# The decay of a Mamba recurrence in a ring of three PSUM banks, with softplus summed by TensorE and three B products lent to GpSimd

## Chip, cores, metric

One Trainium2 chip, one core. The metric is the device time of the whole program in microseconds, the median of the runs; lower is better.

## What is computed

The program runs two layers over a batch of 4 images (128 channels, 64 x 64 = 4096 positions). Layer 0 sorts patches by a score, projects them, runs a selective state-space recurrence and sorts them back; layer 1 is attention over normalised queries and keys, and a mixture of experts. The change touches the recurrence alone and the projection ahead of it:

```python
dbc = xc @ x_proj_w.T                       # dt_low (8), B (16), C (16) for each position
dt = jax.nn.softplus(dt_low @ dt_proj_w.T + dt_proj_b)
dA = jnp.exp(dt[..., None] * A)             # 256 channels x 16 states
dBx = dt[..., None] * Bc[:, :, None, :] * xc[..., None]
h = dA_t * h + dBx_t                        # over 4096 positions
y_t = einsum('bds,bs->bd', h, C_t)
y = y + D * xc;  y = y * silu(z)
```

## The kernel before

A loop over the 4 images runs seven stages; each stage is a block in which every engine has its own instruction queue, tied to the others by counting semaphores. An engine works its queue strictly in order.

The recurrence (`scan`) holds the 256 channels as two halves of 128 partitions and the positions as 8 chunks of 512 columns. Per image it goes over the chunks, in each over the 16 states, and in each state over the two halves. One state takes:

- TensorE (L846, L850) spreads row B of this state over 128 partitions into a PSUM bank, and row C into another, from three bf16 pieces that add up to the fp32 value;
- ScalarE (L870) makes the decay exp(dt x A) of each half in PSUM: four banks, so that decay s, h may be written once the scan of two states before has read its bank; then it copies C to SBUF (L873);
- VectorE (L923, `inject`) multiplies u = dt x xc (SBUF) by B (PSUM) for both halves, 1024 columns, and runs the hardware scan of each half (L941). The queue's order is scan of half 0, injection of the next state, scan of half 1;
- GpSimd (L898) keeps the last column of h for the next chunk, and (L901) multiplies h by C into a separate buffer `g`;
- TensorE (`total`, L838) adds these products into the two Y banks by identity matmuls, four states late, and opens each chunk with two matmuls of D (L836). All of these are fp32, two passes each;
- VectorE's `finish` (L929) multiplies Y by silu(z), once a chunk, after state 2 of the next.

Beside this, the steps of the next chunk are made in between (`Steps`): the dt projection (L593), |v| and relu(v) (L600, L601), exp(-|v|) (L605), 1 + e (L610), a rounding rest on VectorE (L626), Ln (L614, with a table load before and another at the next decay), two GpSimd passes that make softplus (L646, L650), GpSimd's u (L653), and the bf16 pieces: ScalarE high (L617) and middle (L621), GpSimd remainder (L636) and low (L640). For chunk 0 the same steps are made inside the stage before, `project`, in which the input projections (L682, L685), a four-tap convolution on VectorE (L760, L763), Silu (L710, L716) and the x projection (L676) go over the chunks.

The functions that the diff touches:

Of the kernel before, what the change touches and what calls it, by code (L numbers as in the profile page):

```python
# [16 lines left out]
HD = DI // 128  # L17
# [542 lines left out]
class Steps:  # L560
# [4 lines left out]
    def __init__(self, k, dt_banks):  # L565
        self.k, self.dt_banks = k, dt_banks
        at = [STEPS_AT]

        def take(cols):
            at[0] += cols  # L570
            return k.at(at[0] - cols, cols)

        self.dt, self.u = [take(HD * CH) for _ in range(2)], [take(HD * CH) for _ in range(2)]
        self.ab, self.onep, self.rx = take(HD * CH), take(HD * CH), take(HD * CH)
        self.rest = self.onep[:, 0:CH]
# [4 lines left out]
        (self.dt_mm, self.ab_s, self.e_s, self.w_s, self.q_s, self.ln_s, self.rx_s, self.l1_s, self.dt_s, self.hi_s, self.mid_s,  # L580
         self.r_s, self.pc_s) = (k.sem(n) for n in (
             "dt_mm", "dt_abs", "dt_exp", "dt_onep", "dt_rest", "dt_ln", "dt_relu", "log1p", "dt_ready", "high_ready",
             "middle_ready", "remainder", "pieces_ready"))

    def credit_first(self, eng):

        for s, n in ((self.dt_mm, HD), (self.ab_s, 2), (self.e_s, 1), (self.w_s, 1), (self.q_s, 1), (self.ln_s, 1), (self.rx_s, 2),
                     (self.l1_s, 1), (self.dt_s, 2), (self.hi_s, 1), (self.mid_s, 1), (self.r_s, 1), (self.pc_s, 1)):
            eng.sem_inc(s, n)

    def tensor_dt(self, pe, c, h):
        k = self.k
        pe.matmul(k.bank(self.dt_banks[h]), k.dtw[:, h * 128:(h + 1) * 128], self.dbc[:, cols_of(c)], start=True, stop=True)\  # L593
            .then_inc(self.dt_mm, 1)

# [11 lines left out]
    def scalar_one_plus(self, act, c):  # L607
        act.wait_ge(self.e_s, c + 1)
        act.wait_ge(self.pc_s, c + 1)
        act.activation(self.onep, self.ab, ACT.Identity, bias=self.k.cols[:, C_ONE:C_ONE + 1]).then_inc(self.w_s, 1)  # L610

    def scalar_log(self, act, c):
        act.wait_ge(self.q_s, c + 1)
        act.activation(self.onep, self.onep, ACT.Ln).then_inc(self.ln_s, 1)  # L614

# [6 lines left out]

    def vector_rounding(self, dve, c):

        dve.wait_ge(self.w_s, c + 1)
        dve.scalar_tensor_tensor(self.ab, self.onep, 1.0, self.ab, ALU.subtract, ALU.subtract).then_inc(self.q_s, 1)  # L626
# [15 lines left out]
    def pool_softplus(self, pool, c, q, part):  # L642

        if part == 0:
            self.pool_wait(pool, self.ln_s, c + 1)
            pool.tensor_tensor(self.onep, self.onep, self.ab, ALU.subtract).then_inc(self.l1_s, 1)  # L646
        if part == 1:
            self.pool_wait(pool, self.l1_s, c + 1)
            self.pool_wait(pool, self.rx_s, c * 2 + 2)
            pool.tensor_tensor(self.dt[q], self.onep, self.rx, ALU.add).then_inc(self.dt_s, 1)  # L650
        if part == 2:
            self.pool_wait(pool, self.dt_s, c * 2 + 1)
            pool.tensor_tensor(halves(self.u[q]), halves(self.dt[q]), self.xc[:, :, cols_of(c)], ALU.mult).then_inc(self.dt_s, 1)  # L653


def project(k):
# [12 lines left out]
    with nc.Block() as block:  # L669
        @block.tensor  # L670
        def _(pe):
# [16 lines left out]
            for c in range(1, 4):  # L688
# [6 lines left out]
            with pe.Fori(4, NCH) as c:  # L695
                inproj(c)
                xproj(c - 1)
# [3 lines left out]
        def _(act):  # L701
# [40 lines left out]
            steps.scalar_one_plus(act, 0)  # L742
            k.ready_table(act, ACT.Silu, 2)
            with act.Fori(4, NCH - 2) as c:
                body(c)
            steps.scalar_log(act, 0)
            body(NCH - 2)
            body(NCH - 1)
# [4 lines left out]
        def _(dve):  # L753
# [13 lines left out]
            with dve.Fori(0, 5) as c:  # L767
                convolve(c)
            steps.vector_rounding(dve, 0)
            with dve.Fori(5, NCH) as c:  # L770
                convolve(c)

        @block.gpsimd
        def _(pool):
# [4 lines left out]
            for part in range(3):  # L779
                if part == 2:  # L780
                    steps.pool_wait(pool, xc_s, HD)
                steps.pool_softplus(pool, 0, 0, part)
# [8 lines left out]
def scan(k):  # L791
# [5 lines left out]
    B_BANK, C_BANK, DA_BANK, Y_BANK = 0, 1, 2, 6  # L797
    steps = Steps(k, (C_BANK, C_BANK))
# [3 lines left out]
    dbx, hb, g = low[0:2], low[2:6], low[6:10]  # L802
    cs = [low[10 + i // 2][:, (i % 2) * CH:(i % 2 + 1) * CH] for i in range(4)]
    assert steps.end <= ARENA
    dt, u, pieces, dt_s, rx_s, pc_s = steps.dt, steps.u, steps.pieces, steps.dt_s, steps.rx_s, steps.pc_s

    b_mm, c_mm, y_mm, da_s, dbx_s, sc_s, hl_s, hc_s, cs_s, fin_s = (k.sem(n) for n in (
        "b_mm", "c_mm", "y_mm", "da_ready", "dbx_ready", "scan_done", "hlast_saved", "hc_ready", "c_copied", "chunk_done"))

    def da(s, h):  # L810

        return k.bank(DA_BANK + HD * (s % 2) + h)
# [15 lines left out]
    with nc.Block() as block:  # L828
        @block.tensor
        def _(pe):  # L830
            def total(c, s):
                pe.wait_ge(hc_s, c * DS + (s + 5))
# [4 lines left out]
                for h in range(HD):  # L837
                    last = pe.matmul(k.bank(Y_BANK + h), k.ident[:, :], halves(g[s % 4])[:, h, :], start=False, stop=s == DS - 1)  # L838
                last.then_inc(y_mm, 1)

            def body(c, q, more):
                pe.wait_ge(pc_s, c + 1)
                for s in range(DS):
                    n = c * DS + s
                    pe.wait_ge(dbx_s, n + 1)
                    pe.matmul(k.bank(B_BANK), k.sel[:, s, :], pieces[q], start=True, stop=True).then_inc(b_mm, 1)  # L846
                    pe.wait_ge(cs_s, n + 1)
                    if more and 1 <= s <= HD:
                        pe.wait_ge(rx_s, c * HD + (s + HD))
                    pe.matmul(k.bank(C_BANK), k.sel[:, DS + s, :], pieces[q], start=True, stop=True).then_inc(c_mm, 1)  # L850
                    if s >= 4:
                        total(c, s - 4)
                    elif not first(c):
                        total(c - 1, s - 4 + DS)
                    if more and s < HD:
                        pe.wait_ge(cs_s, n + 2)
                        steps.tensor_dt(pe, c + 1, s)
            chunks(body, pe)
            for s in range(DS - 4, DS):
# [3 lines left out]
        def _(act):  # L863
            def body(c, q, more):
                act.wait_ge(dt_s, c * 2 + 1)
                for s in range(DS):
                    n = c * DS + s
                    for h in range(HD):
                        act.wait_ge(sc_s, c * (2 * DS) + (2 * s + h + 5))
                        act.activation(da(s, h), halves(dt[q])[:, h, :], ACT.Exp, scale=k.amat[:, h, s:s + 1]).then_inc(da_s, 1)  # L870
                    act.wait_ge(c_mm, n + 1)
                    act.wait_ge(hc_s, n + 1)
                    act.activation(cs[s % 4], k.bank(C_BANK), ACT.Copy).then_inc(cs_s, 1)  # L873


                    if more and s == 0:
                        steps.scalar_high(act, c + 1, 1 - q)
                    if more and s < HD:
                        steps.scalar_abs(act, c + 1, s)
                    if more and s == 2:  # L880
                        steps.scalar_exp(act, c + 1)
                    if more and s == 3:
                        steps.scalar_middle(act, c + 1, 1 - q)
                    if more and s == 7:
                        steps.scalar_one_plus(act, c + 1)
                    if more and s == 10:
                        steps.scalar_log(act, c + 1)
            chunks(body, act)

        @block.gpsimd  # L890
        def _(pool):
# [3 lines left out]
            def body(c, q, more):  # L895
                for s in range(DS):
                    wait(sc_s, c * (2 * DS) + (2 * s + 2 + 8))
                    pool.tensor_copy(k.hlast[:, s, :, :], halves(hb[s % 4])[:, :, CH - 1:CH]).then_inc(hl_s, 1)  # L898
                    wait(cs_s, c * DS + (s + 2))
                    wait(y_mm, c * DS + (s + 1))  # L900
                    pool.tensor_tensor(halves(g[s % 4]), halves(hb[s % 4]), cs[s % 4].unsqueeze(1).broadcast_to([128, HD, CH]),  # L901
                                       ALU.mult).then_inc(hc_s, 1)
                    if more and s == 0:
                        steps.pool_remainder(pool, c + 1, 1 - q)
                    if more and s == 5:
                        steps.pool_low(pool, c + 1, 1 - q)
                    if more and s in (10, 11, 12):
                        steps.pool_softplus(pool, c + 1, 1 - q, (10, 11, 12).index(s))

            pool.memset(k.hlast[:, :, :, :], 0.0).then_inc(k.sem("h_zero"), 1)  # L910
            pool.wait_ge(k.sem("h_zero"), 1)
            pool.sem_inc(hl_s, DS)
            pool.sem_inc(hc_s, 4)
# [3 lines left out]
        def _(dve):  # L917
            def inject(c, q, s):
                if s == 0:
                    dve.wait_ge(dt_s, c * 2 + 2)  # L920
                dve.wait_ge(b_mm, c * DS + (s + 1))
                dve.wait_ge(sc_s, c * (2 * DS) + (2 * s + 6))
                dve.tensor_tensor(halves(dbx[s % 2]), halves(u[q]), k.bank(B_BANK).unsqueeze(1).broadcast_to([128, HD, CH]),  # L923
                                  ALU.mult).then_inc(dbx_s, 1)

            def finish(c):

                dve.wait_ge(y_mm, c * DS + (DS + 4))
# [3 lines left out]
            def body(c, q, more):  # L932
                inject(c, q, 0)
                for s in range(DS):
                    n = c * DS + s
                    dve.wait_ge(hl_s, n + (DS - 3))
                    dve.wait_ge(hc_s, n + 1)
                    dve.wait_ge(dbx_s, n + 2)
                    for h in range(HD):
                        dve.wait_ge(da_s, c * (2 * DS) + (2 * s + h + 1))  # L940
                        dve.tensor_tensor_scan(halves(hb[s % 4])[:, h, :], da(s, h), halves(dbx[s % 2])[:, h, :],  # L941
                                               k.hlast[:, s, h, :], ALU.mult, ALU.add).then_inc(sc_s, 1)
                        if h == 0 and s < DS - 1:
                            inject(c, q, s + 1)
                    if more and s == 8:
                        steps.vector_rounding(dve, c + 1)
                    if s == 2 and not first(c):
# [4 lines left out]
            dve.sem_inc(cs_s, 1)  # L952
            dve.sem_inc(sc_s, 8)
            dve.sem_inc(fin_s, 1)
            dve.sem_inc(y_mm, 4)
# [771 lines left out]
```

## Time and profile before

| | us |
|---|---|
| median of 3 runs (range) | 5882.98 (5876.63 to 5884.37) |
| the profiled execution, its time | 5884.61 |
| its span | 5882.9 |
| VectorE busy | 5070.9 (86%) |
| TensorE busy | 4708.2 (80%) |
| ScalarE busy | 3751.1 (64%) |
| GpSimd busy | 1666.3 (28%) |
| mean granted TensorE clock | 0.940 of full |

Times are microseconds from the span's start. PE is TensorE, DVE VectorE, ACT ScalarE, POOL GpSimd. Busy shares are over the whole program; the recurrence is four stretches of some 475 us, one for each image. The first runs from about 222 to 698.

### The profile page before, as it was taken

What the parts mean: (1) busy time and instruction counts of PE and PEld (TensorE: products, weight loads), DVE (VectorE), ACT (ScalarE), POOL (GpSimd) and SP (SyncE); (2) the same over time, 40 slices, a digit from 0 to 9 for tenths busy, and PEclk for the clock granted to TensorE, in tenths of its full rate; (3) what the DMA queues carried; (4) which work ended last, traced back from release to release, by engine and by line L of the source; (5) the groups of instructions that cost most, each with busy time, mean ns of one, the idle gap of its engine ahead of it and who ended that gap; (6) DMA issues with size and microseconds to landing.
All of it is one profiled execution on the core that took longest, in us unless ns stands there. A gap on an engine that the chain in (4) does not pass through costs nothing. (4 is left out here: it accounts for less than half of the span.)

```text
span 5882.9 us, 100771 instructions
## 1 busy us (share of the span) xinstructions
PE 4708.2 (80%) x33880; PEld 1953.7 (33%) x33880; DVE 5070.9 (86%) x6502; ACT 3751.1 (64%) x4897; POOL 1666.3 (28%) x1274
## 2 busy tenths in 40 slices
PE   5776779998777777999867777799986677779997
PEld 3222433333322243333332224333343222433334
DVE  6799779998689977999878997799987899679998
ACT  3666468883466646888346663688924666378882
POOL 1488600000048860000004885000000588500000
PEclk9899989999889998999988999899988899989998
DMA  1000020000000002000000000200000000020000
GB/s 38 0 1 0 15 62 9 9 5 22 22 0 1 0 15 62 9 9 5 22 22 0 1 0 15 62 9 9 5 22 22 0 1 0 15 62 9 9 5 15
DMA packets 41626, 87.14 MB, mean 15 GB/s; under 512 B 11672, under 2 KB 27872, under 8 KB 38112
## 3 DMA queue, kind: packets, MB, share of 16 engines
q1 hardware_dynamic: 41184, 81.11, 5.2%
q8 instruction: 294, 4.82, 0.3%
q14 instruction: 148, 1.21, 0.1%
HBM read 26.55 MB, written 8.39 MB: 6 GB/s over the span
## 5 line engine op out<-in xcount | busy, mean ns | idle before, releaser
L1296 ACT ACTIVATE arena<-ps 128x1024 f32<-128x1024 f32 x2048 | 1912.8, 1027 | 258.9 <-PE ps L1261 241.3
L1311 DVE TENSOR_TENSOR arena<-arena 128x1024 f32<-128x1024 f32 x1664 | 1907.8, 1218 | 35.9 <-ACT arena L1296 30.6
L941 DVE TENSOR_TENSOR_SCAN arena<-ps,hlast,arena 128x512 f32<-128x512 f32 x1024 | 1259.4, 1266 | 5.2 <-DVE arena L923 3.2
L901 POOL TENSOR_TENSOR arena<-arena 128x1024 f32<-128x1024 f32 x512 | 1206.8, 2357 | 25.0 <-issue 2.1
L1261 PE MATMUL ps<-arena 128*32 128x512 f16 x16384 | 1093.4, 383 | 118.2 <-issue 47.2
L1244 PE MATMUL ps<-arena 128*32 128x512 f32 x8192 | 1087.4, 609 | 46.0 <-DVE arena L1316 38.1
L870 ACT ACTIVATE ps<-arena,amat 128x512 f32<-128x512 f32 x1024 | 691.9, 688 | 505.1 <-DVE arena L941 504.3
L838 PE MATMUL ps<-arena,ident 128*128 128x512 f32 x2048 | 980.3, 602 | 7.7 <-POOL arena L901 7.7
L1261 PEld LDWEIGHTS ps<-arena 128*32 128x32 f16 x16384 | 470.7, 97 | 975.3 <-issue 650.9
L1619 POOL MEMSET arena<- 128x1024 f32 x4 | 3.8, 956 | 2694.4 <-POOLq L101 2694.4
L923 DVE TENSOR_TENSOR arena<-arena,ps 128x1024 f32<-128x1024 f32 x512 | 611.2, 1194 | 53.8 <-PE ps L846 53.8
L846 PE MATMUL ps<-arena,sel 128*128 128x512 bf16 x512 | 204.8, 400 | 432.3 <-DVE arena L923 418.7
L838 PEld LDWEIGHTS ps<-arena,ident 128*128 128x128 f32 x2048 | 395.8, 194 | 350.2 <-issue 276.2
L1244 PEld LDWEIGHTS ps<-arena 128*32 128x32 f32 x8192 | 213.4, 110 | 471.4 <-ACT arena L1296 246.1
L873 ACT ACTIVATE arena<-ps 128x512 f32<-128x512 f32 x512 | 297.6, 581 | 29.2 <-PE ps L850 28.6
L846 PEld LDWEIGHTS ps<-arena,sel 128*128 128x128 bf16 x512 | 49.8, 97 | 793.6 <-DVE arena L923 737.9
L1665 DVE SCALAR_TENSOR_TENSOR arena<-ps,arena 128x128 f32<-128x128 f32 x1024 | 273.1, 342 | 1.4 <-PE ps L1570 0.2
L1570 PE MATMUL ps<-expw,arena 128*128 128x512 f32 x512 | 248.4, 611 | 10.1 <-DVE arena L1634 8.3
L850 PE MATMUL ps<-arena,sel 128*128 128x512 bf16 x512 | 201.4, 393 | 58.1 <-ACT arena L601 36.3
L486 PE MATMUL ps<-arena 128*128 128x512 f32 x512 | 230.6, 611 | 18.3 <-DVE arena L346 18.3
L898 POOL COPY hlast<-arena 128x2 f32<-128x2 f32 x512 | 118.7, 232 | 319.6 <-DVE arena L941 319.6
L1233 PE MATMUL ps<-arena,ones 128*32 128x512 f32 x1536 | 203.6, 603 | 3.2 <-DVE arena L1311 2.0
(245 smaller groups left out, 4387.5 us busy)
## 6 DMA issues: line engine op xcount, KB each, us to landing
arena<-x SPq DMA_DIRECT2D x32, 512.0 KB, 5.4
arena<-arena SPq DMA_DIRECT2D x64, 256.0 KB, 6.0
arena<-arena SPq DMA_DIRECT2D x64, 224.0 KB, 5.8
arena<-arena SPq DMA_DIRECT2D x28, 512.0 KB, 3.5
arena<-pe SPq DMA_DIRECT2D x256, 32.0 KB, 1.8
out<-arena SPq DMA_DIRECT2D x8, 1024.0 KB, 3.9
expw<-L_ffn_expert_w SPq DMA_DIRECT2D x1, 512.0 KB
wqkv<-L_attn_W_qkv SPq DMA_DIRECT2D x1, 192.0 KB
```

The lines of the kernel that those rows point to most:

```text
L838: last = pe.matmul(k.bank(Y_BANK + h), k.ident[:, :], halves(g[s % 4])[:, h, :], start=False, stop=s == DS - 1)
L846: pe.matmul(k.bank(B_BANK), k.sel[:, s, :], pieces[q], start=True, stop=True).then_inc(b_mm, 1)
L870: act.activation(da(s, h), halves(dt[q])[:, h, :], ACT.Exp, scale=k.amat[:, h, s:s + 1]).then_inc(da_s, 1)
L873: act.activation(cs[s % 4], k.bank(C_BANK), ACT.Copy).then_inc(cs_s, 1)
L901: pool.tensor_tensor(halves(g[s % 4]), halves(hb[s % 4]), cs[s % 4].unsqueeze(1).broadcast_to([128, HD, CH]), ALU.mult).then_inc(hc_s, 1)
L923: dve.tensor_tensor(halves(dbx[s % 2]), halves(u[q]), k.bank(B_BANK).unsqueeze(1).broadcast_to([128, HD, CH]), ALU.mult).then_inc(dbx_s, 1)
L941: dve.tensor_tensor_scan(halves(hb[s % 4])[:, h, :], da(s, h), halves(dbx[s % 2])[:, h, :], k.hlast[:, s, h, :], ALU.mult, ALU.add).then_i ...
L1244: last = pe.matmul(k.ps[32 * h:32 * h + 32, O * CH:(O + 1) * CH], v[:, j * 128 + 32 * h:j * 128 + 32 * h + 32], probs[(2 * j + h // 2) % 8 ...
L1261: last = pe.matmul(k.ps[32 * t:32 * t + 32, (2 * group[p] + e) * CH:(2 * group[p] + e + 1) * CH], ks[:, h, j * 128 + 32 * t:j * 128 + 32 * ...
L1296: act.activation(probs[p % 8], k.bank(2 * group[p], 2 * CH), ACT.Exp, scale=SCALE / SPLIT ** 2).then_inc(exp_s, 1)
L1311: dve.tensor_tensor(acc[p % 2], acc[p % 2], probs[p % 8], ALU.add).then_inc(acc_s, 1)
L1665: dve.scalar_tensor_tensor(tile, k.bank(expert_bank(i, hb), C, e * C), gate[:, i, hb * HE + e:hb * HE + e + 1], tile, ALU.mult, ALU.add).t ...
```

## The change

- The decay goes through a ring of three PSUM banks (position 2s + h modulo 3; the last of a chunk takes bank 1), so a decay may be written when the scan three positions before has read its bank (two at the chunk's first).
- The freed bank X takes the dt projection, the sums of softplus and three lent B rows. TensorE now adds relu(v), e, 1 - (1 + e) and Ln(1 + e) by identity matmuls (`tensor_sum`, fp32, eight a chunk); ScalarE makes the third of these in an extra pass and copies the sums to SBUF as dt. VectorE's rounding pass and two GpSimd passes go.
- For states 6, 10 and 15 ScalarE copies the spread B to SBUF and GpSimd makes the product u x B (in its queue after states 1, 4 and 11); VectorE injects the other 13.
- GpSimd multiplies h by C in place, in a ring of eight h buffers; the totals run six states late, the finish comes after state 4, and C is spread and copied two states late. ScalarE saves the last column of h two states late.
- In `project` the loops over chunks are unrolled on TensorE and ScalarE, Ln follows its exponential directly, the sums stand after chunk 5's matmuls and the copies of dt after chunk 6.

The diff, cut to its core:

```diff
+    def tensor_sum(self, pe, c, q, h, parts):
+        def add(t, n):
+            return pe.matmul(bank, k.ident[:, :], halves(t)[:, h, :], start=n == 0, stop=n == 3)
+        if 0 in parts:
+            pe.wait_ge(self.rx_s, c * HD + HD)
+            add(self.rx, 0)
+        if 1 in parts:
+            pe.wait_ge(self.e_s, c + 1)
+            add(self.ab, 1)
+        if 2 in parts:
+            pe.wait_ge(self.m_s, c + 1)
+            add(self.dt[q], 2)
+        if 3 in parts:
+            pe.wait_ge(self.ln_s, c + 1)
+            add(self.onep, 3).then_inc(self.sum_mm, 1)
+    def scalar_one_minus(self, act, c, q):
+        act.wait_ge(self.w_s, c + 1)
+        act.activation(self.dt[q], self.onep, ACT.Identity, scale=-1.0, bias=self.k.cols[:, C_ONE:C_ONE + 1]).then_inc(self.m_s, 1)
+    def scalar_dt(self, act, c, q, h):
+        act.wait_ge(self.sum_mm, c * HD + (h + 1))
+        act.activation(halves(self.dt[q])[:, h, :], self.k.bank(self.dt_banks[h]), ACT.Copy).then_inc(self.dt_s, 1)
-    def vector_rounding(self, dve, c):
...
+    LOANED = {6: (2, 1), 10: (3, 4), 15: (11, 11)}
+    da_ring = [p % 3 for p in range(HD * DS - 1)] + [1]
...
+            def side(c, q, s, more):
+                if more and s == 0:
+                    if not first(c):
+                        pe.wait_ge(lent_s, c * NL)
+                    steps.tensor_dt(pe, c + 1, 0)
+                if more and s == 1:
+                    pe.wait_ge(rx_s, c * HD + (HD + 1))
+                    steps.tensor_dt(pe, c + 1, 1)
+                if s in spread_at:
...
+                    pe.matmul(k.bank(X_BANK), k.sel[:, p, :], pieces[q], start=True, stop=True).then_inc(lent_mm, 1)
+                if more and s in (4, 5, 6):
+                    if s == 4:
+                        pe.wait_ge(lent_s, lent(c, loans[1]) + 1)
+                    steps.tensor_sum(pe, c + 1, 1 - q, 0, {4: (0, 1), 5: (2,), 6: (3,)}[s])
+                if more and s in (8, 9):
+                    if s == 8:
+                        pe.wait_ge(dt_s, c * HD + (HD + 1))
+                    steps.tensor_sum(pe, c + 1, 1 - q, 1, {8: (0, 1), 9: (2, 3)}[s])
             def body(c, q, more):
                 pe.wait_ge(pc_s, c + 1)
                 for s in range(DS):
+                    if s not in LOANED:
+                        pe.wait_ge(dbx_s, c * OWN + (owned(s) + 1))
+                        pe.matmul(k.bank(B_BANK), k.sel[:, s, :], pieces[q], start=True, stop=True).then_inc(b_mm, 1)
+                    side(c, q, s, more)
+                    if s >= CLATE:
+                        spread_c(c, s - CLATE, q)
...
+                    if s >= LATE:
+                        total(c, s - LATE)
...
             # ScalarE, state s
+                        back = 2 if s == 0 else 3
+                        act.wait_ge(sc_s, c * (2 * DS) + (2 * s + h - back + 9))
                         act.activation(da(s, h), halves(dt[q])[:, h, :], ACT.Exp, scale=k.amat[:, h, s:s + 1]).then_inc(da_s, 1)
+                        if h == 0:
+                            act.wait_ge(sc_s, c * (2 * DS) + (2 * s + 6))
+                            act.activation(k.hlast[:, (s - 2) % DS, :, :], halves(hb[(s - 2) % RING])[:, :, CH - 1:CH], ACT.Copy).then_inc(hl_s, 1)
+                    (copy C of s - 2; the lent copy at 2, 3, 11; for the next chunk: abs and relu at 0, 1; exp at 2;
+                     one plus at 3; one minus at 4; Ln at 5; high at 6; dt half 0 at 7; middle at 8; dt half 1 at 10)
             # GpSimd, state s
+                    pool.tensor_tensor(halves(hb[s % RING]), halves(hb[s % RING]), cs[s % 4].unsqueeze(1).broadcast_to([128, HD, CH]),
+                                       ALU.mult).then_inc(hc_s, 1)
+                    if s in inject_at:
+                        p = inject_at[s]
+                        wait(lent_s, lent(c, p) + 1)
+                        pool.tensor_tensor(halves(dbp[loans.index(p) % 2]), halves(u[q]), bs[loans.index(p) % 2].unsqueeze(1).broadcast_to([128, HD, CH]),
+                                           ALU.mult).then_inc(lent_dbx, 1)
+                    (remainder after state 6, low after 8, u after 9)
```

## Rows read from the trace of the kernel before

**Rows 1.** The page, part 1: busy us, share of the span, instructions.
```profile
PE 4708.2 (80%) x33880; PEld 1953.7 (33%) x33880; DVE 5070.9 (86%) x6502; ACT 3751.1 (64%) x4897; POOL 1666.3 (28%) x1274
```
**Rows 2.** Stretches: length; busy PE, PEld, DVE, ACT, POOL; PEclk; DMA share; GB/s.
```profile
230.00:235.00 5.00, 3.51 (x5) 0.86 (x5) 3.46 (x4) 2.84 (x6) 3.64 (x3) 0.50 0.01 2
...
403.00:461.00 58.00, 40.72 (x104) 15.52 (x104) 57.94 (x50) 37.90 (x60) 49.59 (x38) 1.00 0.00 1
```
**Rows 3.** Waits of VectorE, 217 to 660: who on whom, us in total, times, longest.
```profile
DVE arena L923 <- PE ps L846: 11.8, 4, 8.2
```
**Rows 4.** Timeline of VectorE: start, us, work [idle before]; the finishes of chunks 0, 6, 7.
```profile
297.01 1.20 DVE L929 TENSOR_TENSOR arena<-ps,arena 128x1024 f32<-128x1024 f32 x1
...
646.22 1.20 DVE L929 TENSOR_TENSOR arena<-ps,arena 128x1024 f32<-128x1024 f32 x1
...
696.46 1.23 DVE L929 TENSOR_TENSOR arena<-ps,arena 128x1024 f32<-128x1024 f32 x1 [4.91 <-PE ps L838]
```
**Rows 5.** Timeline, all engines, one state of a steady chunk.
```profile
390.61 2.35 POOL L901 TENSOR_TENSOR arena<-arena 128x1024 f32<-128x1024 f32 x1
391.07 2.45 DVE L941 TENSOR_TENSOR_SCAN arena<-ps,hlast,arena 128x512 f32<-128x512 f32 x2
...
391.21 0.39 PE L846 MATMUL ps<-arena,sel 128*128 128x512 bf16 x1 [1.16 <-DVE arena L923]
...
391.65 1.88 PE L838 MATMUL ps<-arena,ident 128*128 128x512 f32 x4
...
392.91 2.36 POOL L650 TENSOR_TENSOR arena<-arena 128x1024 f32<-128x1024 f32 x1
...
393.44 1.19 DVE L923 TENSOR_TENSOR arena<-arena,ps 128x1024 f32<-128x1024 f32 x1
...
394.55 2.45 DVE L941 TENSOR_TENSOR_SCAN arena<-ps,hlast,arena 128x512 f32<-128x512 f32 x2
```
**Rows 6.** Timeline of VectorE at a chunk's edge.
```profile
285.15 1.19 DVE L923 TENSOR_TENSOR arena<-arena,ps 128x1024 f32<-128x1024 f32 x1
286.54 1.28 DVE L941 TENSOR_TENSOR_SCAN arena<-ps,hlast,arena 128x512 f32<-128x512 f32 x1 [0.20 <-DVE arena L923]
```
**Rows 7.** Timeline of ScalarE around Ln, and the scans beside it.
```profile
436.12 0.58 ACT L873 ACTIVATE arena<-ps 128x512 f32<-128x512 f32 x1
...
436.71 1.28 ACT L614 ACT_TABLE_LOAD   x1
...
438.01 1.06 ACT L614 ACTIVATE arena<-arena 128x1024 f32<-128x1024 f32 x1
...
440.38 1.30 ACT L870 ACTIVATE ps<-arena,amat 128x512 f32<-128x512 f32 x2
...
442.10 0.68 ACT L870 ACTIVATE ps<-arena,amat 128x512 f32<-128x512 f32 x1
442.28 2.45 DVE L941 TENSOR_TENSOR_SCAN arena<-ps,hlast,arena 128x512 f32<-128x512 f32 x2
...
443.59 0.69 ACT L870 ACTIVATE ps<-arena,amat 128x512 f32<-128x512 f32 x1 [0.81 <-DVE arena L941]
```
**Rows 8.** Timeline of TensorE: the D matmuls and the total behind them.
```profile
414.80 1.98 PE L836 MATMUL ps<-arena,dmat 128*128 x4 [1.89 <-DVE arena L929]
...
416.62 1.88 PE L838 MATMUL ps<-arena,ident 128*128 128x512 f32 x4
```
**Rows 9.** Timeline: a small GpSimd piece; a one-column activation.
```profile
427.80 1.15 POOL L640 TENSOR_TENSOR arena<-arena 32x512 bf16<-32x512 f32 x1
...
177.70 0.20 ACT L107 ACTIVATE small<-ones 128x1 f32<-128x1 f32 x1
```
**Rows 10.** Timeline of VectorE in the projection: convolutions of chunks 5 and 6.
```profile
194.29 4.06 DVE L763 SCALAR_TENSOR_TENSOR arena<-arena,taps  x6
200.90 2.04 DVE L760 TENSOR_SCALAR arena<-arena,taps  x2 [2.54 <-ACT arena L705]
202.86 8.24 DVE L763 SCALAR_TENSOR_TENSOR arena<-arena,taps  x6
```

More of the change, by code:

```diff
@@ L574, in __init__ @@
         self.ab, self.onep, self.rx = take(HD * CH), take(HD * CH), take(HD * CH)
-        self.rest = self.onep[:, 0:CH]
+        self.rest = take(CH)
         self.pieces = [take(CH // 2).bitcast(BF16) for _ in range(2)]
@@ L687, in _ @@
             inproj(0)
-            for c in range(1, 4):
+            for c in range(1, NCH):
                 inproj(c)
@@ L694, in _ @@
                         steps.tensor_dt(pe, 0, h)
-            with pe.Fori(4, NCH) as c:
-                inproj(c)
-                xproj(c - 1)
+                if c == 5:
+                    for h in range(HD):
+                        steps.tensor_sum(pe, 0, 0, h, (0, 1, 2, 3))
             xproj(NCH - 1)
@@ L778, in _ @@
             steps.pool_low(pool, 0, 0)
[L779 to L782, printed above, removed]
+            steps.pool_wait(pool, xc_s, HD)
+            steps.pool_u(pool, 0, 0)
     k.clear()
@@ L843, in body @@
                 for s in range(DS):
[L844 to L852, printed above, removed]
-                    elif not first(c):
[L854 to L857, printed above, removed]
+                    if s not in LOANED:
[4 more added lines that the diff above has]
+                        spread_c(c, s - CLATE, q)
+                    elif not first(c):
+                        spread_c(c - 1, s - CLATE + DS, 1 - q)
+                    if s >= LATE:
+                        total(c, s - LATE)
+                    elif not first(c):
+                        total(c - 1, s - LATE + DS)
             chunks(body, pe)
-            for s in range(DS - 4, DS):
+            for s in range(DS - CLATE, DS):
+                spread_c(NCH - 1, s, 1)
+            for s in range(DS - LATE, DS):
                 total(NCH - 1, s)
@@ L863, in _, with copy_c, copy_lent @@
         def _(act):
+            def copy_c(c, s):
+                n = c * DS + s
+                act.wait_ge(c_mm, n + 1)
+                if s >= 4 or not first(c):
+                    act.wait_ge(hc_s, n - 3)
+                act.activation(cs[s % 4], k.bank(C_BANK), ACT.Copy).then_inc(cs_s, 1)
+            def copy_lent(c, p):
+                act.wait_ge(lent_mm, lent(c, p) + 1)
+                i = loans.index(p)
+                if i or not first(c):
+                    act.wait_ge(lent_dbx, lent(c, p) - (1 if i else 0))
+                act.activation(bs[i % 2], k.bank(X_BANK), ACT.Copy).then_inc(lent_s, 1)
@@ L883, in body @@
                         steps.scalar_middle(act, c + 1, 1 - q)
[L884 to L887, printed above, removed]
+                    if s == 10:
+                        steps.scalar_dt(act, c + 1, 1 - q, 1)
+            act.wait_ge(k.sem("h_zero"), 3)
             chunks(body, act)
+            for s in range(DS - CLATE, DS):
+                copy_c(NCH - 1, s)
```

170 lines of the change are left out of this document (98 added, 72 removed).

## The prediction

> **What bounds the kernel now.** I read the page first: VectorE is the busiest engine over the span, TensorE next [rows 1]. A share over stages with different limits decides nothing, so I cut out the stage that the change touches by its times. In a steady chunk of the recurrence VectorE is busy 57.94 us of 58.00, TensorE 40.7, ScalarE 37.9, GpSimd 49.6, and TensorE's clock is granted in full (2.4 GHz); in the first chunk it is granted at half (1.2 GHz) [rows 2]. The waits of VectorE over seven and a half chunks are four waits for a B bank, 11.8 us in all, the longest 8.2 before the first injection; so 3.6 us fall inside the first chunk and nothing later [rows 3]. VectorE sets the time of the recurrence.
>
> The timeline gives the beat: 349.21 us between the finishes of chunk 0 and chunk 6, six chunks, 58.20 each [rows 4]. A state takes 3.48 us of VectorE: a scan every 1.18, an injection every 1.12 [rows 5]. At a chunk's edge the first scan waits 0.27 longer for its own injection [rows 6]. 32 scans, 16 injections, the finish, the rounding pass and the edge: 37.76 + 17.92 + 1.12 + 1.12 + 0.27 = 58.19. The count closes, so what is taken from VectorE is saved, unless another wait takes its place.
>
> Other prices. TensorE: 0.22 for a B or C spread (B and C between 391.21 and 391.65), ready 0.42 after its start (0.39 and a hand-over); a state's total of two fp32 matmuls 1.72, so 0.86 for one [rows 5]; the D matmuls 1.82 [rows 8]. GpSimd: 2.30 for a 1024-column pass [rows 5], for a small piece 1.15, or 1.10 with the overlap that lets passes of 2.35 start 2.30 apart [rows 5, 9]. ScalarE: two decays take 1.24 (1.30 less the overlap), and the copy of C costs 0.48 (440.38 to 442.10 is two decays and the copy), Ln 1.07 and a table load 1.29 (438.01 to 440.38 is Ln and the load back) [rows 7]; a one-column activation at most 0.20 [rows 9]. A scan releases ScalarE 0.13 after the next could start: the scan of 442.28 releases the exp of 443.59 [rows 7].
>
> **VectorE's part.** Three of 16 injections and the rounding leave: 3 x 1.12 + 1.12 = 4.48. New work: 53.7 a chunk. This is a gain only if the other three engines keep the order.
>
> **Loads of the others.** GpSimd: 16 products, 3 injections, u: 20 x 2.30, two pieces 2.2: 48.2 (its copies of the last column leave; two of three softplus passes leave; the in-place product I price as now, 2.30). TensorE: 38.1 before (16 x (0.44 + 1.72) + 1.82 + two dt matmuls 1.72), plus 8 sum matmuls x 0.86 = 6.9: 45. ScalarE: 32 x 0.62 + 16 x 0.48 + 16 x 0.20 + two loads 2.6, one extra pass 1.07 (taken at Ln's price), five more copies 2.4 and the old softplus passes: about 43. All are under 53.7, so no engine's load becomes the bound. What can stop VectorE is order.
>
> **Where order bites: state 6.** I set t = 0 where VectorE could leave the first scan of state 4 and lay the queues side by side. VectorE wants: injection 5 to 1.12, scan to 2.30, finish of the chunk before (now at state 4) to 3.42, the two scans of 5 to 5.78, first scan of 6 to 6.96 (6 is lent, no injection), then injection 7, which needs B 7.
> ScalarE: second decay of 5 at 0.14 (three banks: it needs that first scan of 4), copy of C 3 to 1.24, Ln's table to 2.53, Ln to 3.60, Exp's table to 4.9, both decays of 6 to 6.2 (in time for 6.96), copy of C 4, which releases at 6.95.
> TensorE stands at state 6 on a wait for Ln, and behind it in its queue are C 4, the D matmuls, total 0 and B 7. From 3.66: 0.86 + 0.22 + 1.82 + 1.72 = 4.62, to 8.28; B 7 ready at 8.70. Injection 7 wanted 6.96: VectorE stalls 1.74. The total 15 of the chunk before, which the finish awaits, comes out at 2.1 in the same laying out, ahead of 2.30: no stall there.
> A second chain gives the same size by another path. GpSimd's product 4 needs the copy of C 4 (6.95); behind it stand lent injection 10, products 5 and 6 and the remainder: 6.95 + 4 x 2.30 + 1.10 + 0.05 = 17.3. ScalarE at state 8 waits for that remainder, and the decays of 9 are queued behind: middle piece 0.5, decay 0.69 and a hand-over: scan 9 at 18.55. VectorE wants it at 6.96 + 5 x 1.18 + 3 x 1.12 = 16.22. So 2.3 us are lost by then whatever TensorE does; 1.74 is already in it, 0.6 comes on top. GpSimd then owes products 7 to 11, the low piece, u and injection 15 (17.2 us from the copy of C 7, about 2.5 after the remainder): it ends about 0.25 before scan 15 wants it. That margin is thin, and behind this work are the products that the next totals need, with several states of slack in the ring of eight. Small misses elsewhere (B 11): 0.1.
> Period: 53.7 + 2.4 = 56.1 to 56.2, against 58.2: a gain of 2.0 in each of six chunks. Bounds: no stall, 53.7; both chains adding instead of overlapping (4.0) and half a microsecond at scan 15, 58.2.
>
> The table switch is where a page and the row differ. The copy at 436.12 ends at 436.70, the load runs to 437.99 and Ln starts at 438.01; so the switch costs the load alone [rows 7]. The Trainium skill (ScalarE: Activation LUTs, What ACT_TABLE_LOAD costs) puts a drain of 1380 ns beside the load of 1283 ns; the trace agrees with the load and shows no drain. By that rule both chains would be up to 2.76 longer, the period 58.9.
>
> **The ends of a batch.** Chunk 0: VectorE saves 4.48, and dt is moved ahead, so that the 3.6 us of early waits mostly go; but no finish covers Ln's tables at state 6 (scan 6 waits about 1 to 3.6), and TensorE is at half clock then [rows 2]: its 4.62 may become 9.2. I take -0.5, between -5 and +4. Chunk 7 has no next step: -3.35, no jam. The tail: now the last finish stands idle 4.91 after the last scan, 5.0 from where it could start [rows 4]. After, C comes two states late: copy of C 13 releases product 13 at -2.1 from the last scan's end, products 13, 14, 15 run to +4.8 and the total takes 1.9: 6.8, so +1.8. Scan stage: -0.5 - 12.0 - 3.35 + 1.8 = -14.05.
>
> **Projection.** Ln moves up beside the first Exp; one pass more; the second switch away from Silu goes: ScalarE about even. TensorE gets 8 passes of sums, 3.44, ahead of the input projection of chunk 6, which the convolution of 6 awaits: I take it as not hidden. Against it, the convolution of chunk 6 took 2.04 and 8.24 where that of chunk 5 took 0.88 and 4.06 [rows 10], while three GpSimd passes ran; two of the three leave, the third may fall on chunk 7 (1.7). Moving the softplus up costs 3.4, its removal lower down returns 1.5, the contention 5.3 - 1.7 = 3.6, the two copies of dt cost 1: 3.4 + 3.4 + 1 - 1.5 - 3.6, about +2.5 a batch. Bounds -4 and +6.
> The Trainium skill (SBUF — State Buffer, Who interferes with whom) says that a VectorE operation with two SBUF inputs and a GpSimd one lock each other out of a shared port. Here the convolution agrees; the scans and injections take one large input from PSUM and kept 1.18 and 1.12 beside GpSimd [rows 5], so I add nothing for GpSimd's lent injections.
>
> **Sum.** (-14.05 + 2.5) x 4 = -46. Against the profiled execution's own 5884.6: 5838.4. It stands 1.6 over the median of the runs, so 5837.
>
> **Rivals.** *VectorE stays full* (0.25): queues slip so that neither chain stops it. For it: the loads are all below 53.7. Against: both chains start at Ln and its two table loads. Then -4.48 x 6, -3 in chunk 0, -3.35, +1.8, projection 0: -31.4 a batch, -126, 5757; partly so, up to 5815.
> *The stalls eat it all* (0.12): the two chains add and scan 15 waits; period 58.2. Then -0.5 - 3.35 + 1.8 + 2.5, about 0: 5885.
> *TensorE's clock falls* (0.05, the other side): at 1.2 GHz the 4.62 us ahead of B 7 become 9.24, period 60.8; with +2.6 x 6, +2 in chunk 0 and the rest as above +18.5 a batch: 5958. It decides from a period of 58.6 (each us of it is worth 24). For it: TensorE is idle 1.9 us before, waiting for Ln. Against: full clock throughout, with a gap of 1.16 in every state now [rows 2, 5].
> *GpSimd is the bound* (0.06): an in-place product 10% dearer adds 2.6 over the two GpSimd chains, period 58.8: 5901.
> *The switch has its drain* (0.02), period 58.9, +2.8 in chunk 0: +7.5 a batch, 5915. The mechanism is a pause of 1.38 between load and activation; the page named above is its source.
> My forecast (2.4 us of stalls, 5837; its own range 5815 to 5862) has 0.50. Under 0.2% (12 us) a change can't be told from none: faster 0.76 (my forecast, the first rival and a sliver of the second), same 0.11, slower 0.13 (the last three). The range 5770 to 5888 holds the first two rivals but for the far end of the one (0.06), and leaves out the three slow ones.
>
> **What would show it.** Right: finishes 56.2 apart; VectorE's waits are for the B bank about 1.7 us at injection 7 and for a decay about 0.6 at scan 9, each chunk; TensorE idle on Ln before sum part 3; ScalarE's middle piece waiting on GpSimd's remainder; last finish 6.8 after the scans. Wrong: a beat of 54 (chains hidden), 2.3-us products grown, waits for a lent injection, a clock below 1 in steady chunks, or a projection that is longer by more than 6 us.

## Result and the profile after

The changed kernel takes 5904.12 us (median of 5 runs, 5902.72 to 5910.99) against 5882.98 us, a ratio of 1.0042 with a 95% interval of 1.0027 to 1.0057. It is slower, where 5837 and a gain were forecast; the time lies outside the range. The profiled execution has a span of 5904.3 us, 21.4 more than before.

The page of the kernel after, part 1 (busy us, share, instructions), beside [rows 1]:

```profile
PE 4911.8 (83%) x34324; PEld 2066.6 (35%) x34392; DVE 4922.7 (83%) x6374; ACT 3920.0 (66%) x5597; POOL 1630.8 (28%) x802
```

VectorE did lose the work that was taken from it: 5070.9 to 4922.7, 148 us. None of that came through. The stretches of three steady chunks and of the middle of the last one in the first image (columns as in [rows 2]):

```profile
345.00:403.00 58.00, 47.42 (x120) 19.22 (x120) 55.23 (x48) 44.28 (x84) 49.93 (x24) 1.00 0.00 1
403.00:461.00 58.00, 48.37 (x118) 19.91 (x120) 53.70 (x47) 43.33 (x81) 48.31 (x23) 0.97 0.00 1
...
654.00:660.00 6.00, 4.23 (x5) 1.85 (x6) 5.16 (x5) 3.50 (x7) 4.03 (x3) 0.57 0.00 1
```

VectorE is no longer full (57.94 of 58 before), and TensorE's granted clock, 1.00 in [rows 2], is 0.97 in some chunks and falls to 0.57 for six microseconds of the last. The timeline of VectorE, its waits and finishes in the same image (L1023 injection, L1047 scan, L1029 finish; in brackets the idle time before, and who ended it), to be read beside [rows 4] and [rows 6]:

```profile
228.24 1.22 DVE L1023 TENSOR_TENSOR arena<-arena,ps 128x1024 f32<-128x1024 f32 x1 [8.06 <-remote]
...
252.58 1.28 DVE L1047 TENSOR_TENSOR_SCAN arena<-ps,hlast,arena 128x512 f32<-128x512 f32 x1 [2.97 <-ACT hlast L952]
257.96 1.22 DVE L1023 TENSOR_TENSOR arena<-arena,ps 128x1024 f32<-128x1024 f32 x1 [4.10 <-PE ps L911]
...
307.98 1.20 DVE L1029 TENSOR_TENSOR arena<-ps,arena 128x1024 f32<-128x1024 f32 x1
...
364.63 1.19 DVE L1029 TENSOR_TENSOR arena<-ps,arena 128x1024 f32 x1
...
371.18 1.22 DVE L1023 TENSOR_TENSOR arena<-arena,ps 128x1024 f32<-128x1024 f32 x1 [1.81 <-PE ps L911]
...
381.24 3.63 DVE L1047 TENSOR_TENSOR_SCAN arena<-ps,hlast,arena 128x512 f32<-128x512 f32 x3 [0.69 <-ACT ps L949]
...
410.22 1.22 DVE L1023 TENSOR_TENSOR arena<-arena,ps 128x1024 f32<-128x1024 f32 x1 [1.55 <-PE ps L911]
...
423.00 1.20 DVE L1029 TENSOR_TENSOR arena<-ps,arena 128x1024 f32 x1
...
635.60 1.20 DVE L1023 TENSOR_TENSOR arena<-arena,ps 128x1024 f32<-128x1024 f32 x1
...
654.43 1.20 DVE L1029 TENSOR_TENSOR arena<-ps,arena 128x1024 f32<-128x1024 f32 x1
...
662.61 1.22 DVE L1023 TENSOR_TENSOR arena<-arena,ps 128x1024 f32<-128x1024 f32 x1 [3.44 <-PE ps L911]
...
704.23 1.23 DVE L1029 TENSOR_TENSOR arena<-ps,arena 128x1024 f32<-128x1024 f32 x1 [11.28 <-PE ps L871]
```

The two waits that the laying out of state 6 foresaw are there, to a tenth of a microsecond: 1.81 for B 7 (forecast 1.74) and 0.69 for the decay of state 9 (forecast 0.6). A beat with these two waits alone, from one finish to the next, is 364.63 - 307.98 = 56.65. But the next is 58.37, and it holds one more wait: 1.55 at 410.22, for B 2. Three other places are worse than forecast: injection 7 of the last chunk (3.44), the last finish (11.28 idle, 4.91 in [rows 4]), and the start, 228.24 where it was 224.09.

First image, term by term, in us against before:

| term | forecast | measured | from |
|---|---|---|---|
| projection, first injection | +2.5 | +4.15 | 228.24 - 224.09 |
| chunk 0, edge to edge | -0.5 | -0.14 | 60.92 - 61.06 |
| chunks 1 to 6, edge to edge | -12.0 | -2.8 | 346.4 - 349.2 |
| chunk 7, to its last scan | -3.35 | +0.2 | 57.3 - 57.1 |
| tail, to the last finish | +1.8 | +6.4 | 11.35 - 4.99 |

In the table an edge is the first injection of a chunk. That is +7.8 for this image. From first injection to last finish the four images take 472.4, 476.5, 476.4 and 474.4 us before and 476.0, 476.1, 476.1 and 476.1 after, so the recurrence is 4.5 us longer in all. From the first input projection to the first injection the images take 73.4, 72.9, 71.3 and 70.4 us before and 77.6, 77.5, 77.4 and 77.4 after, 21.7 in all: the larger part of the loss. The stages that the change leaves alone were 4.8 us shorter in this execution.

### The profile page after: what moved, and what is told of

The parts are those of the page before. It is cut to its first block and busy times, and to the rows that moved or that the text cites. A ratio compares the mean times of both kernels' runs of the same rounds, so it can differ in the third digit from the quotient of the medians.

```text
span 5904.3 us, 102171 instructions
## 1 busy us (share of the span) xinstructions
PE 4911.8 (83%) x34324; PEld 2066.6 (35%) x34392; DVE 4922.7 (83%) x6374; ACT 3920.0 (66%) x5597; POOL 1630.8 (28%) x802
## 5 line engine op out<-in xcount | busy, mean ns | idle before, releaser
L995 POOL TENSOR_TENSOR arena<-arena 128x1024 f32<-128x1024 f32 x512 | 1197.1, 2351 | 345.7 <-ACT arena L934 188.3
L1047 DVE TENSOR_TENSOR_SCAN arena<-ps,hlast,arena 128x512 f32<-128x512 f32 x1024 | 1254.3, 1265 | 39.4 <-ACT hlast L952 20.6
L871 PE MATMUL ps<-arena,ident 128*128 128x512 f32 x2048 | 981.4, 604 | 23.1 <-ACT arena L934 22.0
L949 ACT ACTIVATE ps<-arena,amat 128x512 f32<-128x512 f32 x1024 | 704.7, 688 | 327.0 <-DVE arena L1047 324.5
L1023 DVE TENSOR_TENSOR arena<-arena,ps 128x1024 f32<-128x1024 f32 x416 | 498.1, 1197 | 129.1 <-PE ps L911 91.0
L871 PEld LDWEIGHTS ps<-arena,ident 128*128 128x128 f32 x2048 | 401.5, 196 | 363.9 <-issue 331.6
L602 PE MATMUL ps<-arena,ident 128*128 128x512 f32 x512 | 262.8, 632 | 68.0 <-ACT arena L638 53.5
L877 PE MATMUL ps<-arena,sel 128*128 128x512 bf16 x472 | 188.1, 398 | 110.3 <-ACT arena L934 110.1
L911 PE MATMUL ps<-arena,sel 128*128 128x512 bf16 x388 | 153.3, 395 | 119.2 <-DVE arena L1023 118.7
L1000 POOL TENSOR_TENSOR arena<-arena 128x1024 f32<-128x1024 f32 x96 | 225.8, 2353 | 0.0
```

Of the source, the lines that this page charges most:

```text
L602: return pe.matmul(bank, k.ident[:, :], halves(t)[:, h, :], start=n == 0, stop=n == 3)
L871: last = pe.matmul(k.bank(Y_BANK + h), k.ident[:, :], halves(hb[s % RING])[:, h, :], start=False, stop=s == DS - 1)
L995: pool.tensor_tensor(halves(hb[s % RING]), halves(hb[s % RING]), cs[s % 4].unsqueeze(1).broadcast_to([128, HD, CH]), ALU.mult).then_inc(hc ...
L1023: dve.tensor_tensor(halves(dbx[owned(s) % 2]), halves(u[q]), k.bank(B_BANK).unsqueeze(1).broadcast_to([128, HD, CH]), ALU.mult).then_inc(d ...
L1047: dve.tensor_tensor_scan(halves(hb[s % RING])[:, h, :], da(s, h), halves(injected)[:, h, :], k.hlast[:, s, h, :], ALU.mult, ALU.add).then_ ...
```

## Experiments

Each edit is on the changed kernel, and each ratio is to the kernel before, run on the same chip (its medians there: 5880.87, 5881.37 and 5885.74). Where a result is set against the changed kernel, that is its 1.0042. That ratio is known to 0.0015 (9 us) either way, so gains of 7 to 11 us (experiments 1, 3, 4 and 7) are hardly clear in the medians; there the lengths and waits in the traces carry the reading.

**1. Fill TensorE in states 12 to 15.**

```diff
+                    if s in (12, 13, 14, 15):
+                        if s == 12:
+                            pe.wait_ge(lent_s, lent(c, loans[-1]) + 1)
+                        for _ in range(4):
+                            pe.matmul(k.bank(X_BANK), k.sel[:, 0, :], pieces[q], start=True, stop=True)
```

> The changed kernel with four extra B spreads at the end of TensorE's states 12, 13, 14 and 15, into bank X, which nobody reads then (16 matmuls of 0.22 us a chunk, in gaps of 1.16 to 1.3 us). Theory (the clock falls because TensorE is too idle ahead of the chunk's edge, so the total and the dt matmul take double and B 2 comes late): the granted clock stays 1.00 in every steady chunk, the 1.55 us wait of VectorE for B 2 goes from the four or five chunks that have it, the beat is 56.7 throughout, and the time falls by some 4.5 x 1.7 x 4 = 30 us to about 5874. Rival (the wait at B 2 is an order wait behind relu(v) and dt): the wait stays and the time is the same or a little longer.

Measured: 5893.78, ratio 1.0019 (1.001 to 1.0027). The time is 10 us under the changed kernel, where 30 were expected. The extra spreads did fill the gaps, but the wait for B 2 stayed in three chunks of the first image (1.55, 1.54, 1.38) and left one. Neither theory: the falls are touched, not cured. Most of what was gained (11.7 of the 14 us by which the four recurrences are shorter) lies in the last chunk, 46.9 us from finish to finish and not 49.8. The timeline and the stretches of TensorE in this run (L911 B, L593 dt, L877 C, L871 total) show where a fall begins:

```profile
402.54 1.88 PE L871 MATMUL ps<-arena,ident 128*128 128x512 f32 x4
405.52 0.39 PE L911 MATMUL ps<-arena,sel 128*128 128x512 bf16 x1 [1.10 <-DVE arena L1028]
406.81 1.73 PE L593 MATMUL ps<-arena,dtw 128*128 x2 [0.89 <-ACT arena L622]
408.33 0.63 PE L877 MATMUL ps<-arena,sel 128*128 128x512 bf16 x1
408.76 2.80 PE L871 MATMUL ps<-arena,ident 128*128 128x512 f32 x4
```

```profile
404.00:405.00 1.00, 0.42 (x1) 0.00 (x0) 1.00 (x2) 0.64 (x2) 1.00 (x2) 1.00 0.00 0
405.00:406.00 1.00, 0.39 (x1) 0.10 (x1) 0.88 (x2) 1.00 (x3) 1.00 (x1) 1.00 0.00 0
406.00:407.00 1.00, 0.19 (x1) 0.20 (x2) 1.00 (x2) 1.00 (x3) 1.00 (x2) 1.00 0.03 8
407.00:408.00 1.00, 1.00 (x2) 0.25 (x2) 1.00 (x2) 1.00 (x3) 1.00 (x1) 0.60 0.00 0
408.00:409.00 1.00, 1.00 (x3) 0.57 (x2) 1.00 (x1) 0.04 (x2) 0.70 (x1) 0.50 0.00 0
```

Before the fall, from 404 to 407, TensorE was busy 1.0 of 3 us: it waited for the first injection to free the B bank (1.10) and for relu(v) (0.89). Then dt, C and the total run at 1.2 GHz, the total in 2.80 instead of 1.88, and B 2 stands behind them.

**2. Fill those two gaps.**

```diff
                 if more and s == 0:
                     if not first(c):
                         pe.wait_ge(lent_s, c * NL)
-                    steps.tensor_dt(pe, c + 1, 0)
+                        for _ in range(4):
+                            pe.matmul(k.bank(X_BANK), k.sel[:, 0, :], pieces[q], start=True, stop=True)
+                    else:
+                        steps.tensor_dt(pe, c + 1, 0)
                 if more and s == 1:
+                    if not first(c):
+                        pe.wait_ge(cs_s, (c - 1) * DS + (DS - 1))
+                        for _ in range(4):
+                            pe.matmul(k.bank(C_BANK), k.sel[:, 0, :], pieces[q], start=True, stop=True)
...
                         total(c - 1, s - LATE + DS)
+                    if more and s == 0 and not first(c):
+                        steps.tensor_dt(pe, c + 1, 0)
```

> The changed kernel with TensorE's two idle gaps at the chunk's edge filled: at state 0 four extra spreads into bank X before C 14 and the dt matmul moved behind the total, at state 1 four extra spreads into the C bank (its copy done) ahead of the wait for relu(v). The fill at states 12 to 15 had left most falls of the clock, and in each of them TensorE was busy 1.0 of the 3 us before the fall. Theory (those gaps let the clock fall): no fall to 1.2 GHz in chunks 2 to 7, no 1.5 us wait for B 2, beat 56.7, 25 to 30 us less than the changed kernel: 5875. Rival (the clock falls for another reason, a limit on work done): the falls stay or grow more, the time is equal or longer.

Measured: 5865.42, ratio 0.9972 (0.9963 to 0.9982): 0.7% under the changed kernel, some 41 us, more than the 25 to 30 expected. In the first image all six beats are 56.7 and the wait for B 2 is in none. Stretches of chunks 3 and 5:

```profile
405.00:463.00 58.00, 50.05 (x133) 20.59 (x132) 55.23 (x48) 44.52 (x84) 49.52 (x24) 1.00 0.00 1
...
521.00:579.00 58.00, 50.04 (x132) 20.42 (x131) 55.15 (x48) 44.69 (x85) 49.59 (x23) 1.00 0.00 0
```

Useless matmuls make the kernel faster, and in chunks 1 to 6 of the first image the clock is at full; the first and the last chunk still have falls (0.94 over the last), so the expectation of none in chunk 7 failed. This edit alone turns the change from a loss into a gain. The four recurrences are 41.0 us shorter: 24.4 in the beats of chunks 1 to 6, as expected, 1.5 in chunk 0 and 15.1 in the last chunk, which the edit doesn't touch. There, in images 2 to 4, the wait at injection 7 is 0.53 and no longer 3.45, and the idle time before the last finish 9.58 and not 11.27; in the first image they are 2.23 and 11.28.

The edit also moves a dt matmul behind the total. That this order alone did it is ruled out by chunk 2 of the changed kernel: it has the same gaps and the dt matmul in its old place, but kept full clock, and has no wait for B 2. TensorE in the changed kernel, chunk 2 and chunk 3:

```profile
347.13 0.39 PE L911 MATMUL ps<-arena,sel 128*128 128x512 bf16 x1 [1.56 <-DVE arena L1023]
348.42 1.12 PE L593 MATMUL ps<-arena,dtw 128*128 x2 [0.89 <-ACT arena L622]
...
349.59 1.88 PE L871 MATMUL ps<-arena,ident 128*128 128x512 f32 x4
...
403.84 0.39 PE L911 MATMUL ps<-arena,sel 128*128 128x512 bf16 x1 [1.48 <-DVE arena L1023]
405.13 1.61 PE L593 MATMUL ps<-arena,dtw 128*128 x2 [0.89 <-ACT arena L622]
...
406.95 2.93 PE L871 MATMUL ps<-arena,ident 128*128 128x512 f32 x4
```

**3. Catch up the totals in the last chunk.**

```diff
+            CATCH = {12: (6, 7), 13: (8,), 14: (9, 10), 15: (11,)}
-                    if s >= LATE:
+                    if not more and s in CATCH:
+                        for t in CATCH[s]:
+                            total(c, t)
+                    elif s >= LATE:
                         total(c, s - LATE)
...
-            for s in range(DS - LATE, DS):
+            for s in range(DS - 4, DS):
                 total(NCH - 1, s)
```

> The changed kernel, but in the last chunk TensorE adds up the totals earlier: totals 6 and 7 at state 12, 8 at 13, 9 and 10 at 14, 11 at 15, so that four and not six stand behind the last C spread. Theory (the finish waits 11.28 us because six totals of 1.72 us follow the last C): the wait falls to GpSimd's last product plus one total, about 7 us, 4.3 less an image, 17 us in all: about 5887. Rival (GpSimd's products set the end): no change.

Measured: 5893.28, ratio 1.0024 (1.0016 to 1.0033), 11 us under the changed kernel. The idle time before the last finish went from 11.28 to 7.8, so TensorE's queue of totals set the end, as expected; 3.5 an image, not 4.3. In the changed kernel, the tail of TensorE's queue in the timeline (the last C, then six totals in 24 passes) reads:

```profile
691.80 0.39 PE L877 MATMUL ps<-arena,sel 128*128 128x512 bf16 x1 [0.69 <-ACT arena L934]
692.03 12.16 PE L871 MATMUL ps<-arena,ident 128*128 128x512 f32 x24
```

**4. Spread B 7 and B 11 ahead.**

```diff
-                    if s not in LOANED:
-                        pe.wait_ge(dbx_s, c * OWN + (owned(s) + 1))
-                        pe.matmul(k.bank(B_BANK), k.sel[:, s, :], pieces[q], start=True, stop=True).then_inc(b_mm, 1)
+                    b = s + 1 if s in (6, 10) else s
+                    if s not in (7, 11, 15):
+                        pe.wait_ge(dbx_s, c * OWN + (owned(b) + 1))
+                        pe.matmul(k.bank(B_BANK), k.sel[:, b, :], pieces[q], start=True, stop=True).then_inc(b_mm, 1)
```

> The changed kernel, but B 7 is spread at TensorE's state 6, ahead of its wait for Ln, and B 11 at state 10 (the B bank is free there, since those states are lent). My account says that a second chain (copy of C 4, four GpSimd passes, the remainder, the middle piece, decay 9) takes what is gained: the 1.8 us wait at injection 7 goes, the wait at scan 9 grows from 0.7 to about 2.4, and the time falls by 0.1 to 0.2 us a chunk, 3 to 10 us in all. Rival (the TensorE queue alone costs the 1.8 us): 1.8 x 28 = 50 us less, about 5854.

Measured: 5895.21, ratio 1.0031 (1.0018 to 1.0043). The wait at injection 7 is gone, the one at scan 9 has grown from 0.69 to 1.85, and two of 0.27 for B 8 and B 9 have come: VectorE, from the finish of chunk 2 on:

```profile
425.84 1.20 DVE L1030 TENSOR_TENSOR arena<-ps,arena 128x1024 f32 x1
...
434.32 1.22 DVE L1024 TENSOR_TENSOR arena<-arena,ps 128x1024 f32<-128x1024 f32 x1 [0.27 <-PE ps L912]
...
438.19 1.22 DVE L1024 TENSOR_TENSOR arena<-arena,ps 128x1024 f32<-128x1024 f32 x1 [0.28 <-PE ps L912]
...
442.46 3.63 DVE L1048 TENSOR_TENSOR_SCAN arena<-ps,hlast,arena 128x512 f32<-128x512 f32 x3 [1.85 <-ACT ps L950]
```

The sum is 2.4, as before (1.81 + 0.69 = 2.5). The other chain, which is shorter by a little, took the whole gain; the rival, 50 us, is out. That the time fell by the 3 to 10 us expected is luck. The six beats of the first image grew from 346.5 to 349.2 us in all, since a wait for B of 1.26 to 2.92 now stands at every chunk's edge but the last; the last chunk shrank from 49.8 to 45.3.

**5. Make the remainder after state 4.**

```diff
-                    if more and s == 6:
+                    if more and s == 4:
                         steps.pool_remainder(pool, c + 1, 1 - q)
```

> The changed kernel, but GpSimd makes the remainder after state 4's lent product and not after state 6, so it is there when ScalarE comes to the middle piece at state 8. Theory: the 0.68 us wait at scan 9 goes, the 1.8 us at injection 7 stays: 0.7 x 28 = 19 us less, about 5885. Rival (something else in ScalarE's queue holds decay 9, or the lent product 15 comes later by as much): no change.

Measured: 5848.25, ratio 0.9944 (0.9932 to 0.9955), 1% under the changed kernel, three times what was expected. The wait at scan 9 is gone and the beat without a fall is 55.6 (419.32 - 363.75), 1.1 less. That accounts for about 26 us. Of the other 29 us by which the four recurrences are shorter, 7 are falls that became fewer, 3 in each image (in the first at 350.97, 463.77, 576.47) where there were 4, 4 are the first chunk, and 18 are the last (45.2 for 49.8), in which the wait at injection 7 is 0.53 for 3.44 and the idle time before the finish 9.58 for 11.28. In the first image the granted clock is 1.00 there. Why a shorter beat should meet fewer falls I didn't test by itself.

**6. Experiments 4 and 5 together.**

> The remainder after state 4 and B 7, B 11 ahead, together. Theory (two chains from Ln, one through TensorE to B 7, one through GpSimd's remainder to decay 9, each hides the other's price; the remainder alone gave 1.1 us a chunk, B ahead alone nothing in the beat): together they give both, the waits at injection 7 and at scan 9 are gone, the beat without a fall of the clock is 53.9 to 54.4, and the time is 1.5 x 28 = 40 us under that of the remainder alone, about 5805. Rival (GpSimd's lent product 15 is the next bound): waits for it of 1 us or more, about 5830.

Measured: 5809.48, ratio 0.988 (0.9863 to 0.9896). The beat is 54.4 (413.51 - 359.11), against 53.7 of plain work. B ahead alone had taken nothing off a beat without a fall (56.74 in experiment 4); on top of the remainder it gives 39 us. So there were two chains from Ln, and each hid what the other cost.

**7. The sums later in the projection.**

```diff
                 inproj(c)
+                if c == 7:
+                    for h in range(HD):
+                        steps.tensor_sum(pe, 0, 0, h, (0, 1, 2, 3))
                 xproj(c - 1)
-                if c == 5:
-                    (the same two sums)
...
+            for h in range(HD):
+                steps.scalar_dt(act, 0, 0, h)          # was after chunk 6's work
             silu_x(NCH - 1)
```

> The changed kernel, but in the projection the eight sum matmuls (16 passes, 7.03 us in one piece) stand after chunk 7's input projection and not ahead of chunk 6's, and the copies of dt after chunk 7's other work. Theory (TensorE's sums delay the input projection of chunk 6 and with it the convolutions by 6.9): the first injection comes 4 to 6 us earlier in each image, 16 to 24 us in all: about 5882. Rival (the sums are hidden, and the later start comes from the softplus that moved up): no change, or later, since dt and u come later.

Measured: 5897.12, ratio 1.0024 (1.0016 to 1.0033). The first injection comes at 224.73, 3.5 us earlier, and not 4 to 6; over the four images the stage is 12.0 us shorter, where 16 to 24 were expected. The convolution of chunk 6 starts at 201.02 and not 207.95, but the sums now delay the x projection: they run from 207.36 to 214.2 ahead of it, and ScalarE waits 7.51 us for it. In the changed kernel the timeline of TensorE and VectorE shows the whole block ahead of chunk 6 (L602 sums, L696 input projection, L776 convolution):

```profile
198.38 7.03 PE L602 MATMUL ps<-arena,ident 128*128 128x512 f32 x16
...
205.25 1.88 PE L696 MATMUL ps<-arena,wx 128*128 128x512 f32 x4
...
207.95 0.88 DVE L776 TENSOR_SCALAR arena<-arena,taps  x2 [7.62 <-ACT arena L719]
```

**8 and 9. All of it, with and without the fill at the edge.**

> All that the runs pointed to, on top of the changed kernel: remainder after state 4, B 7 and B 11 ahead, the two gaps at the chunk's edge filled, totals caught up in the last chunk, the sums later in the projection. If the terms are separate they add: from the remainder and B ahead (5809), less 14 for the projection (3.5 us an image), less 10 to 14 for the tail (3.5 us an image), less 0 to 8 for the few falls of the clock that are left: 5775 to 5785. Rival (with the stalls gone GpSimd's lent product 15 or the sums bind instead): the beat stays above 55, 5800 or more.

> The same without the fill at the chunk's edge (and the dt matmul back in its place). It tells the fill's worth once the order stalls are gone: if the clock still falls at chunk edges in some chunks, each fall costs 1.3 to 1.6 us of VectorE's wait for B 2, and this kernel is 5 to 15 us over the one with the fill; if no falls are left, the two are equal.

Measured: 5769.29, ratio 0.981 (0.9794 to 0.9826), and 5771.36, ratio 0.9803 (0.979 to 0.9817). The terms add up to what was written down, or a little better: they are 1.9% and 2.0% faster than the kernel before, and 2.3% and 2.4% than the changed one. Beats of the one with the fill are 54.3 to 54.5 throughout. Once the order stalls are gone the medians can't tell the fill's worth: one chunk of each image still has a fall without it (in the first a beat of 55.90, 413.88 to 469.78), which is 6 us in the four recurrences of the profiled executions, while the medians differ by 2 us. So the fill is worth 41 us with the stalls and some 6 beside their cure.

## Why the prediction was wrong

**What held.** The bound, the closed count of 58.19, VectorE's saving (4.48 a chunk; its busy time fell by 148 us in 32 chunks, 4.6 each), the price of 2.30 for the in-place and the lent products (means of 2.351 and 2.353 us for one against 2.357 before), the table load without a drain (in the changed kernel Ln ends at 366.01, the load runs from 366.03 to 367.31, the decay starts at 367.33), and the two chains of state 6 with their 1.74 and 0.6. The 56.65 of a chunk without a fall stands 0.45 over my 56.2: 0.16 is in the two waits, the rest I have not traced. Experiments 4 to 6 show that the chains are what I said, and that the second was worth more than the 0.6 at its end.

**"TensorE's clock falls ... Against: full clock throughout, with a gap of 1.16 in every state now."** This step failed. I had the right mechanism, gave it 0.05, and looked for it in the wrong place: ahead of B 7 in steady chunks, where it did not occur (1.82 in nearly every chunk). It came at the chunk's edge, where the change put the dt matmul behind a wait for relu(v), and where state 15, being lent, has no B: 0.75 us of work from 402 to 405, the 3 us before the fall (1.0 of 3 in experiment 1). A steady 1.16 of idle in 3.48 said nothing about such a stretch. Experiment 2 shows its price: 24 us in the beats, and 15 more in the last chunks, whose clock changed with it. In the first image four beats of 58.1 to 58.4 against 56.7, 6.4 us, are the larger part of the 9.2 by which chunks 1 to 6 missed.

**"Chunk 7 has no next step: -3.35, no jam."** The chunk kept the jam at injection 7 (3.44) though no sum stands there: D and total 0 took 3.75 and 3.04 at 1.2 GHz, after 1.88 us of waiting for the finish:

```profile
655.77 3.75 PE L869 MATMUL ps<-arena,dmat 128*128 128x512 f32 x4 [1.88 <-DVE arena L1029]
...
659.31 3.04 PE L871 MATMUL ps<-arena,ident 128*128 128x512 f32 x4
```

That took all that VectorE had saved. At full clock the same work leaves a wait of 0.53 (experiment 5, where D and the total take 1.96 and 1.88), so 2.9 of the 3.44 are the clock. Less work on TensorE isn't enough to explain the fall: experiment 5 has no more of it in this chunk.

**"The total takes 1.9: 6.8, so +1.8."** The tail was sized by GpSimd's last product and one total. I did not count the six totals that the lateness leaves in TensorE's own queue behind the last C: 6 x 1.72 = 10.3. Measured were 12.16, since the clock fell once more there (granted 0.59 and 0.56 from 692 to 696); in experiment 5, at full clock, the six took 10.46 and the idle time was 9.58. The lateness and that fall cost 4.6 an image more than forecast; experiment 3 took 3.5 of it back.

**"TensorE gets 8 passes of sums, 3.44."** A slip: eight matmuls of two passes are 16, and 7.03 us; in the chunk I had priced the same eight at 6.9. The convolution of chunk 6 came 7.05 later (207.95, 200.90 in [rows 10]); experiment 7 gives 6.93 of it back. It was partly offset, as the contention went (4.06 for 8.24) and the first convolution began 1.67 earlier: +4.15 in place of +2.5. In the later images the stage lost more, 4.6 to 7.0, since there the kernel before had been quicker (70.4 in the last).

The sum of the misses in the first image is 1.65 + 0.4 + 9.2 + 3.5 + 4.6 = 19.3 us. Over all four the recurrence was forecast at 56 us less and came out 4.5 longer, the projection at 10 longer and came out 21.7. What stays open: why the clock falls at one chunk's edge and not at the next, with the same 1.5 and 0.9 us gaps (chunk 2 kept full clock, chunks 3 to 6 did not). The kernel before has it too, in its later images: waits of 1.2 to 1.3 for B at a chunk's edge (at 1943.60 behind a granted clock of 0.50 from 1940 to 1942), which make them 2 to 4 us longer than its first.

## To carry to other kernels

When work moves to an engine that has room, count its longest thin stretch and not its load: a loop with short idle times in every round can still have one place where it waits twice, and there the clock may fall for the next few microseconds of work. Two chains that leave one instruction and come back at different places hide each other; a fix of one alone proves nothing about its worth, so lay out both before trying either. An added lateness is paid at the end of every pass, in the queue of the engine that has to catch up.

## Not expected of the hardware

TensorE's clock went to 1.2 GHz in the midst of work in which it is busy 48 of 58 us, with no idle gap above 2 us in the chunk (1.5 at most at the edge where it fell), after a stretch of 3 us with 0.75 us of matmuls; eight spreads of 0.22 us in the gaps around it kept the clock at 2.4 GHz in chunks 1 to 6 of the first image. The same gaps did not bring a fall in chunk 2.
